# Four graph layers on one core: a group's softmax sums one unit later with longer rings, layer 3's biases added by VectorE and its norm scales made by GpSimd, layer 2's two norms sharing their small steps

## The reference

```python
x = norm(x + L0(x))   # q, k, v of the edges; score = exp(clip(k[src].q[dst] / sqrt(32), -5, 5)); sum(v*score) / sum(score)
x = norm(x + L1(x))   # z = (1+eps)*x + sum(x[src]); relu(z@W1+b1)@W2+b2; r = z+x; relu(norm(r)*gamma+beta)
x = norm(x + L2(x))   # h = x@W; e = leaky(a_src[src]+a_dst[dst]), self loops too; softmax over dst; + bias; norm*ln_w+ln_b
x = norm(x + L3(x))   # q,k,v with biases; k,v of an edge + edge_attr@We; softmax over dst; sum(v*alpha) + x@Ws + bs
```

## Time and profile before

| | |
|---|---|
| median of 3 runs | 5001.02 us (4994.6 to 5005.99) |
| the profiled execution | 4998.33 us, span 4996.6 us |
| TensorE busy | 4563.9 us, 91% of the span |
| TensorE's weight loads | 3506.0 us, 70% |
| VectorE busy | 3986.5 us, 80% |
| ScalarE busy | 2805.1 us, 56% |
| GpSimd busy | 2476.3 us, 50% |

### The profile page before, as it was taken

One profiled execution on the slowest core, in us unless ns is written; L12 is line 12 of the kernel. 1 busy time (PEld: TensorE's weight loads), 2 busy tenths in 40 slices (PEclk: granted clock), 3 DMA queues, 4 the chain that ended last, 5 costly groups with the idle time before them and its releaser, 6 DMA issues. The chain is left out here.

```text
span 4996.6 us, 90737 instructions
## 1 busy us (share of the span) xinstructions
PE 4563.9 (91%) x21673; PEld 3506.0 (70%) x21722; DVE 3986.5 (80%) x13147; ACT 2805.1 (56%) x6326; POOL 2476.3 (50%) x2462
## 2 busy tenths in 40 slices
PE   4999998779999999999888888888799999699998
PEld 3666664448888888888767777777566666577777
DVE  4777778979999999999859999999855555567666
ACT  1787886545555555555547777777611111366565
POOL 3555551237777777777466666666365554000000
PEclk8999996569999999999979999999899999899999
DMA  6777778954444444444468888787555554677775
GB/s 138 210 225 222 223 223 257 298 187 135 150 152 153 149 148 152 153 153 148 143 184 252 244 244 244 243 243 243 183 172 163 163 164 146 193 228 228 223 228 160
DMA packets 911233, 970.10 MB, mean 194 GB/s; under 512 B 104899, under 2 KB 867258, under 8 KB 910892
## 3 DMA queue, kind: packets, MB, share of 16 engines
q1 hardware_dynamic: 500692, 471.58, 32.9%
q10 hardware_dynamic: 327416, 315.35, 18.6%
q0 software_dynamic: 82784, 179.41, 12.3%
HBM read 654.56 MB, written 363.57 MB: 204 GB/s over the span
## 5 line engine op out<-in xcount | busy, mean ns | idle before, releaser
L1186 POOL DMA_INDIRECT nodes_near_rows<-hh_d,source_row x392 | 394.9, 1007 | 401.3 <-DVE nodes_weighted L1403 292.6
L586 POOL DMA_INDIRECT layer_xg<-in_x,edge_rows x392 | 386.7, 987 | 358.5 <-PE layer_t_ps L627 241.5
L884 POOL DMA_INDIRECT nodes_near_rows<-x_d,nodes_cur x392 | 419.0, 1069 | 238.2 <-POOL nodes_cur L879 170.8
L1542 POOL DMA_INDIRECT edges_xg<-x_d,edge_rows x392 | 372.9, 951 | 264.3 <-PE edges_x_ps L1568 172.6
L485 ACT ACTIVATE nodes_x<-nodes_outer_rows,nodes_outer_shift,nodes_outer_rstd 128x256 f32<-128x256 f32 x784 | 428.0, 597 | 61.1 <-issue 51.4
L1597 ACT ACTIVATE edges_xT<-edges_x_ps 128x512 f32<-128x512 f32 x196 | 117.1, 597 | 524.7 <-PE edges_x_ps L1568 524.7
L1806 PE MATMUL nodes_agg<-w_s,nodes_xT 128*128 128x256 f32 x1568 | 405.5, 381 | 0.0
L1004 PE MATMUL nodes_h_ps<-w_h,nodes_x2T 128*128 128x272 f32 x1568 | 392.2, 393 | 8.1 <-ACT nodes_x2T L1081 8.1
L660 PE MATMUL layer_agg<-layer_msg,layer_hot 128*128 128x264 f32 x784 | 314.2, 540 | 73.5 <-issue 65.7
L642 PE MATMUL layer_kv_ps<-w_kv,layer_xT 128*128 128x512 f32 x784 | 372.3, 597 | 1.0 <-DVE layer_made L751 1.0
L994 PE MATMUL nodes_out_ps<-w_b,nodes_hid 128*128 128x256 f32 x1568 | 371.2, 380 | 1.4 <-DVE nodes_inner_rows L925 0.8
(11 more groups left out here) (223 smaller groups left out, 12341.3 us busy)
## 6 DMA issues: line engine op xcount, KB each, us to landing
nodes_xin<-x_d SPq DMA_DIRECT2D x588, 256.0 KB, 3.8
layer_msg<-msg_d SPq DMA_DIRECT2D x392, 132.0 KB
hh_d<-nodes_hh ACTq DMA_DIRECT2D x196, 264.0 KB, 4.1
nodes_msg<-msg_d SPq DMA_DIRECT2D x392, 132.0 KB, 3.1
x_d<-layer_y ACTq DMA_DIRECT2D x196, 256.0 KB, 3.8
x_d<-nodes_x2b ACTq DMA_DIRECT2D x196, 256.0 KB, 3.5
nodes_hin<-hh_d SPq DMA_DIRECT2D x196, 256.0 KB, 3.9
x_d<-nodes_x ACTq DMA_DIRECT2D x196, 256.0 KB
```

The costliest lines, as they stand in the source:

```text
L586: gp.indirect_dma_start(out=xg[:, c % 8, k, :], out_offset=None, in_=x, in_offset=bass.IndirectOffsetOnAxis(ap=edge_rows[:, c, k:k + 1], a ...
L884: gp.indirect_dma_start(out=near_rows[:, r, h, :], out_offset=None, in_=x1_d, in_offset=bass.IndirectOffsetOnAxis(ap=cur[:, r, h:h + 1], a ...
L1186: gp.indirect_dma_start(out=near_rows[:, u % NR, h, :], out_offset=None, in_=hh_d, in_offset=bass.IndirectOffsetOnAxis(ap=source_row[:, 2 ...
L1542: gp.indirect_dma_start(out=xg[:, c % 8, k, :], out_offset=None, in_=x3_d, in_offset=bass.IndirectOffsetOnAxis(ap=edge_rows[:, c, k:k + 1] ...
```

## The change

- prepare: the attention columns, `gin`, the identity into `w3_s` and the split of biases leave this stage, as do the seven loads for them and for layer 3's biases. Only layer 2's bias is still split. VectorE converts the targets first and the sources behind the first mask.
- layer0: that work is done in twelve pieces, `weights(piece)`, one per VectorE step from step 61 on; its inputs are three loads at the head of ScalarE's queue. The DMAs into `pairs` go from the head of SP's queue to units 8 to 15, and their users from step 11 to step 29. `w0_kv` and `w0_q` are freed after the stage.
- nodes2: from the group's sum on, every lag grows by one. `NR` goes from 16 to 20, `HOT` from 18 to 20, `XR` from 9 to 8. The inner norm of one unit and the outer norm of the unit three behind it share one square root, one reciprocal and one shift; the root stands behind `e_row` in ScalarE's queue, the reciprocal behind `own` in VectorE's, the shift behind the inner statistics. The copy of `near_score` is two where a group wraps around the ring.
- edges3: layer 3's biases are loaded as rows at the head of SP's queue, the bias matmul is gone, and VectorE adds `kv_bias` in PSUM ahead of the join.
- nodes3: the bias matmul is gone and VectorE adds `root_bias` to `agg` in place, ahead of the statistics. GpSimd makes the one-hots and, in four small operations with a power of −0.5, the norm's scale and shift; ScalarE's root is gone. The group's sum and shares come a step later, and the transpose of the shares goes from the head of TensorE's step at lag 15 to the end of the step at lag 16.

The diff, cut:

```diff
-                for k in (1, 0):
-                    ve.wait_ge(edges_in[k], 48)
-                    nc.vector.tensor_copy(ends_f[:, k, :, :], ends_c[:, k, :, :]).then_inc(cast, 1)
-                for k in (1, 0):
-                    last = nc.vector.tensor_copy(pairs[:, :, :, k], ends_c[:, k, :, :])
-                last.then_inc(paired, 1)
+                ve.wait_ge(edges_in[1], 48)
+                nc.vector.tensor_copy(ends_f[:, 1, :, :], ends_c[:, 1, :, :]).then_inc(cast, 1)
+                nc.vector.tensor_copy(pairs[:, :, :, 1], ends_c[:, 1, :, :])
...
+                    if mask is below_lo:
+                        ve.wait_ge(edges_in[0], 48)
+                        nc.vector.tensor_copy(ends_f[:, 0, :, :], ends_c[:, 0, :, :]).then_inc(cast, 1)
+                        nc.vector.tensor_copy(pairs[:, :, :, 0], ends_c[:, 0, :, :]).then_inc(paired, 1)
...
-                link(nc.vector.tensor_tensor(b3[:, 0:D], b3[:, 0:D], rows["L2_gnn_ln_b"][0:3, :], ALU.subtract))
...
-        MASKS = U0 + 6
+        MASKS, WEIGHTS = U0 + 24, U0 + 56
...
-                sp.wait_ge(lists_out, 16)
-                for h in range(H):
-                    sp.dma_start(pairs[h * 2 * GU:(h + 1) * 2 * GU, 0:WHOLE, :],
-                                 windows[0:WHOLE * 2 * GU, :].rearrange("(g w) x -> w g x", w=2 * GU)).then_inc(pairs_in, 16)
-                    sp.dma_start(pairs[h * REST:(h + 1) * REST, WHOLE, :], windows[WHOLE * 2 * GU:TILES, :]).then_inc(pairs_in, 16)
                 for u in range(UNITS):
+                    if 8 <= u < 8 + H:
+                        h = u - 8
+                        sp.wait_ge(lists_out, 16)
+                        sp.dma_start(pairs[h * 2 * GU:(h + 1) * 2 * GU, 0:WHOLE, :],
+                                     windows[0:WHOLE * 2 * GU, :].rearrange("(g w) x -> w g x", w=2 * GU)).then_inc(pairs_in, 16)
+                        sp.dma_start(pairs[h * REST:(h + 1) * REST, WHOLE, :], windows[WHOLE * 2 * GU:TILES, :]).then_inc(pairs_in, 16)
...
+                for k, name in enumerate(("L2_gnn_att_src", "L2_gnn_att_dst")):
+                    act.dma_start(att[:, k, :], row(a[name], D)).then_inc(more_in, 16)
+                for k, name in enumerate(split_biases):
+                    act.dma_start(b3[:, k * D:(k + 1) * D], row(a[name], D, 3)).then_inc(more_in, 16)
...
+                def weights(piece):
+
+                    if piece == 0:
+                        ve.wait_ge(more_in, (2 + BV) * 16)
+                        link(nc.vector.tensor_tensor(b3[:, 0:D], b3[:, 0:D], rows["L2_gnn_ln_b"][0:3, :], ALU.subtract))
+                        nc.vector.tensor_scalar(gin[:, :], gin[:, :], 1.0, None, ALU.add)
+                    elif piece <= 2 * KC:
+                        k, j = (piece - 1) // 2, (piece - 1) % 2
+                        link(nc.vector.tensor_tensor(wprod[:, :], w2_h[:, k, 0:D], att[:, j, :], ALU.mult))
+                        link(nc.vector.tensor_reduce(watt[:, k, j * H:(j + 1) * H],
+                                                     wprod[:, :].rearrange("p (h c) -> p h c", h=H), axis=AX.X, op=ALU.add))
...
+                    if WEIGHTS <= s < WEIGHTS + 12:
+                        weights(s - WEIGHTS)
...
-        NR, HR, XR, WR, HOT, LATER = 16, 5, 9, 4, 18, 12
+        NR, HR, XR, WR, HOT, LATER = 20, 5, 8, 4, 20, 12
...
-                    g = at(14)
+                    g = at(15)
...
-                    tops, shares = (g // GU if g is not None and g % GU == 0 else None for g in (at(12), at(13)))
-                    u = at(19)
-                    if u is not None:
-                        norm_invert(ve, inner, (None, 8, u))
-                    u = at(22)
-                    if u is not None:
-                        norm_invert(ve, outer, (None, 8, u))
-                    u = at(19)
-                    if u is not None:
-                        norm_shift(ve, inner, (None, 8, u))
-                    u = at(22)
-                    if u is not None:
-                        norm_shift(ve, outer, (None, 8, u))
+                    tops, shares = (g // GU if g is not None and g % GU == 0 else None for g in (at(12), at(14)))
...
+                    if at(20) is not None or at(23) is not None:
+                        b, of = two_norms(s - 1, at(20), at(23))
+                        ve.wait_ge(rooted, s - 19)
+                        nc.vector.reciprocal(rstd[:, b, of, :], dev[:, b, of, :]).then_inc(inverted, 1)
...
+                    if at(20) is not None or at(23) is not None:
+                        b, of = two_norms(s - 1, at(20), at(23))
+                        ve.wait_ge(inverted, s - 19)
+                        nc.vector.scalar_tensor_tensor(shift[:, b, of, :], moments[:, b, of, :, 0], -1.0, rstd[:, b, of, :], ALU.mult, ALU.mult)\
+                            .then_inc(shifted, 1)
...
-                        norm_root(act, inner, (None, 8, u))
...
-                        norm_root(act, outer, (None, 8, u))
+                    if at(19) is not None or at(22) is not None:
+                        b, of = two_norms(s, at(19), at(22))
+                        if at(19) is not None:
+                            act.wait_ge(inner_merged, at(19) + 1)
+                        if at(22) is not None:
+                            act.wait_ge(outer_merged, at(22) + 1)
+                        nc.scalar.activation(dev[:, b, of, :], moments[:, b, of, :, 1], ACT.Sqrt, bias=eps_ln[:, :]).then_inc(rooted, 1)
...
+                for k, name in enumerate(("L3_gnn_bk", "L3_gnn_bv")):
+                    sp.dma_start(kv_bias[:, k * D:(k + 1) * D], row(a[name], D)).then_inc(bias_in, 16)
+                sp.dma_start(q_bias[:, :], row(a["L3_gnn_bq"], D)).then_inc(bias_in, 16)
...
-                        nc.tensor.matmul(kv_ps[r][:, :], ones3[:, :], bias3[:, 2 * D:4 * D], start=True, stop=False)
...
+                    c = at(2)
+                    if c:
+                        of_chunk = kv_ps[ring(c, 4)]
+                        ve.wait_ge(kv_done, num(c) + 1)
+                        nc.vector.tensor_tensor(of_chunk[:, :], of_chunk[:, :], kv_bias[:, :], ALU.add).then_inc(kv_biased, 1)
...
+            @blk.gpsimd
+            def _(gp):
+                link = chained(gp, small)
+                link(gp.memset(minus_half[:, :], -0.5))
+
+                def body(s, at):
+                    u = at(16)
+                    if u is not None:
+                        if u >= 4:
+                            gp.wait_ge(summed, u - 3)
+                        for h in range(2):
+                            last = gp.tensor_scalar(hot[:, u % 4, h, :], iota[:, :], target_rel[:, 2 * u + h:2 * u + h + 1], None, ALU.is_equal)
+                        last.then_inc(hot_ready, 1)
+                    u = at(20)
+                    if u is not None:
+                        b = u % 4
+                        gp.wait_ge(ln["merged"], u + 1)
+                        if u >= 4:
+                            gp.wait_ge(ln["normed"], u - 3)
+                        link(gp.tensor_scalar(ln["spread"][:, b, :], ln["moments"][:, b, :, 1], LN_EPS, None, ALU.add))
+                        link(gp.tensor_tensor(ln["rstd"][:, b, :], ln["spread"][:, b, :], minus_half[:, :], ALU.pow))
+                        link(gp.tensor_tensor(ln["back"][:, b, :], ln["moments"][:, b, :, 0], ln["rstd"][:, b, :], ALU.mult))
+                        gp.tensor_scalar(ln["shift"][:, b, :], ln["back"][:, b, :], -1.0, None, ALU.mult).then_inc(ln["shifted"], 1)
+                run_units(UNITS, 20, body)
...
-                        norm_invert(ve, ln, (None, 8, u))
-                    u = at(15)
-                    if u is not None:
-                        if u >= 4:
-                            ve.wait_ge(summed, u - 3)
-                        one_hot_halves(ve, (None, 8, u), 4, hot, hot_ready)
-                    u = at(20)
-                    if u is not None:
-                        norm_shift(ve, ln, (None, 8, u))
-                    u = at(16)
+                        if u == 0:
+                            ve.wait_ge(bias_in, 16)
+                        ve.wait_ge(summed, u + 1)
+                        nc.vector.tensor_tensor(in_halves(agg[u % 4]), in_halves(agg[u % 4]), both(root_bias), ALU.add).then_inc(based, 1)
...
-                    g = group(15)
-                    if g is not None:
-                        n = of_group(g) * H
-                        pe.wait_ge(share_ready, g + 1)
-                        if g:
-                            pe.wait_ge(weighed, GU * g)
-                        nc.tensor.transpose(share_ps[:, 0:n], share[0:n, :], ident[0:n, 0:n]).then_inc(share_turned, 1)
...
-                            nc.tensor.matmul(to, ones3[:, :], bias3[:, D:2 * D], start=False, stop=False)
...
+                    g = group(16)
+                    if g is not None:
+                        n = of_group(g) * H
```

(5 more changed lines are left out.)

260 lines of the change are left out of this document (144 added, 116 removed).

## The result

The changed kernel takes 4829.9 us (median of 4 runs, 4822.56 to 4838.49), the kernel before 4999.9 us beside it (4 runs): a ratio of 0.966, 95% interval 0.9641 to 0.968. The forecast was 4811 us. The profiled execution took 4828.96 us, span 4827.2.

The account below looks back on a forecast made before the run. TensorE was taken to bound layer0's first part, edges3 and most of nodes3, VectorE layer0's second part and, as busiest, nodes2. 4998.3 − 16 − 13 − 42 − 89 − 30 = 4808, plus 2.7 to the median: 4811 us, range 4745 to 4875.

Parts of the forecast that it names:

- Both terms: prepare: VectorE's tail moves to layer0 (−12 us), and its idle wait for the source list goes (−4 us).
- The mechanism and the size: layer0: pairs copies leaving SP's queue head end TensorE's stops of 4.1 and 7.9 us; −13 us with clock recovery.
- The matmul's price: edges3: dropping the 512-column bias matmul saves 0.216 us in each of 196 chunks, 42.4 us.
- Part (c): nodes3: VectorE stays about level, ScalarE loses the square root, and the replacement on GpSimd is hidden below 3.03 us.
- part (b): nodes3: share transpose at the end of a 3 us step ends TensorE's 1.9 us stop per group, 46 us.
- TensorE's own 24.5 us a group: nodes3: TensorE's issue time per group, two share transposes included, against 28.4 us before; 95 us over 24.5 groups.
- GpSimd's 2.4 us per unit: nodes3: estimated time of the compares and small norm operations queued on GpSimd, bounds 1.0 to 4.2 us.
- The rival that decides from 3.03: nodes3: GpSimd's chain becomes the bound from 3.03 us per unit; at 4.5 us the kernel takes 5099 us; chance 0.06.
- Two remain, taken at 0.2: nodes2: of VectorE's four small norm operations (0.37 us) two remain at 0.2, its normal step going from 4.35 to 4.18.
- The normal step: nodes2: TensorE's own 4.38 us step, through ScalarE's copies of the one work bank, stays, so normal steps gain nothing.
- clock holds: nodes2 rival: TensorE's clock no longer falls, 74 us gained, 44 more than forecast; kernel 4767 us; chance 0.2.
- nodes2 gives nothing: Part of a rival: nodes2's heavy steps stay as long and layer0's traffic only moves; about 4851 us; chance 0.17.

Follow-up runs that it names:

- the last pair of runs: Fastest nodes2 order (own, reciprocal late, merges early) on the changed kernel, without and with layer0's pairs copies back at SP's queue head: 4753.8 and 4764.6 us.
- add waits: Changed kernel, but GpSimd's nodes2 add waits for VectorE's shift and both statistics merges stand right behind the scaling by ln_w: 4791.5 us, ratio 0.9579.
- own late: Changed kernel, but in nodes2 VectorE issues inner statistics, reciprocal, outer statistics, shift, then own, with both merges behind the ln_w scaling: 4820.9 us, ratio 0.9581.
- merges early: Changed kernel's nodes2 with both statistics merges right behind the ln_w scaling, run only with other edits; with GpSimd's add waiting for the shift 4791.5 us.
- the waiting add alone: Changed kernel with one wait more: GpSimd's nodes2 add begins only after VectorE's shift of the same step; 4833.4 us, ratio 0.9611.

## Why the prediction was right, and where it was not

**prepare** (−16, measured −18.1). Both terms held. VectorE begins on the tiles of the targets at 9.74 instead of 16.36, and its last conversion, of the first edges, starts at 33.01 instead of 39.82: 6.8 us, where I counted 4 and bounded by 7.2. The loads and the barrier behind it take 4.2 us, where I took 3.

**layer0** (−13, measured −11.8). The mechanism and the size held: 10.9 us go with the copies into pairs, by the last pair of runs. What the work moved from prepare costs there was not measured by itself.

**edges3** (−42, measured −38.0). The matmul's price held: zeros put back cost 42.0 (196 x 0.216 is 42.3, not 42.4). What was missing is at the head. TensorE begins 8.3 us after the barrier instead of 6.8, and its first k, v matmuls take 3.27 us instead of 1.88: in the stage's first 16 us the granted clock is 0.50, and it was 0.66 before. The three bias loads start beside the gathers there; that they are what holds the first gathers back was not tested.

```profile
3573.20 0.42 SPq L1594 DMA_DIRECT2D edges_q_bias<-in_L_gnn_bq  x1
...
3580.27 1.09 PE L1616 MATMUL edges_x_ps<-ident,edges_xg 128*128 128x128 f32 x4 [24.14 <-DMA edges_xg<-x_d,edge_rows]
...
3585.06 3.27 PE L1631 MATMUL edges_kv_ps<-w_kv,edges_xT 128*128 128x512 f32 x4
```

**nodes3** (−89, measured −91.6). The sum is right, two of its steps are not. The bias matmuls (43) are confirmed at 42.5 us, and taking the share transpose back to its old place (46) costs 40 to 41. Part (c) I had costed at nothing, hidden work in exchange for hidden work. Taken back alone it costs 43 us: VectorE's step again begins with a wait for the root, its weighted product comes late, and TensorE stops for it ahead of the share transpose, at the new place too (19.0 us in 540), and for the copy of x behind the root (7.5). So part (b)'s "the stop goes", because a step is longer than 1.9 us, was not true of the place alone; it needed (c). The three prices add up to some 126 us and the stage gained 92, because each is what one edit is worth when the other two are there, and (b) and (c) end the same stop. The sum came out by some luck, because I had bounded it by TensorE's own 24.5 us a group, and 24.45 is where it went. GpSimd's 2.4 us per unit became 2.55 (500.1 / 196), and with what lies between its operations 2.86: in 540 us it waited only 34.6 for a merge, (540 − 34.6) / 177. The power alone takes 0.72 of it. The rival that decides from 3.03 was nearer than the 0.06 said.

**nodes2** (−30, measured −10.9). Here the failed step is one that I had in hand. I had cited the Trainium skill ("SBUF — State Buffer", section "Who interferes with whom") against part (c), found the two-input operations of nodes3 harmless, and did not ask the same of nodes2, where GpSimd's add of x reads SBUF for 1.26 us in every step and the edit moved VectorE's shift, both of whose inputs are in SBUF, from ahead of `own` to behind it, that is from before GpSimd's add to inside it. The trace and the runs agree with that rule: 0.715 us against 0.144, 85 us of VectorE's time, and nodes2 shorter by 43 us (add waits) and 50 us (own late), merges early in both, when the overlap is taken away. Of these the waiting add alone gives 1.1 us a group (42.3 to 41.2), some 27 us; the rest comes with the other edits of those kernels and at the stage's ends. The trace of the kernel before had the sign too, in the 16 long shifts above. "Two remain, taken at 0.2" is the term that was mis-sized: they take 0.16 and 0.62 us (103.3 / 168).

The rest of the working in nodes2 stands worse than its total. The forecast had a group shorter by 1.4 us and its light steps as long as before. By the table above the three lightest steps got 0.9 us longer together, and the other five 1.9 us shorter. The normal step was not held at 4.38 us by TensorE: it went up to 4.68 with the stretched shift, and some went down to 4.12 where the add waits. The lag and the rings alone were worth some 24 us. The clock was wrong as well: it was to fall once a group as before, and it fell 10 times in 21 groups. That is half of what the rival "clock holds" asked for, and the stage was not shorter for it than forecast. The range held the time because its upper side had room for "nodes2 gives nothing", and the forecast is near because prepare, edges3 and nodes3, 147 of its 190 us, came out at 148 together.

What remains open: why `own` behind the statistics and the reciprocal with it shortens the other five steps by 2 us a group was not taken apart, nor which of lag and rings gives the first 24 us.

## What to carry to other kernels

When an edit moves a small VectorE operation, write down what GpSimd does at its new place. In this kernel an operation of four elements with both inputs in SBUF ended with GpSimd's add, 0.57 us late as a rule in the changed kernel (0.715 against 0.144) and up to 1.5 us late in the kernel before (1.70 against 0.16); away from that add it took 0.14 to 0.16. Beside the issue of a gather on GpSimd it was mostly short (312 of 323 shifts in nodes2 of the kernel before; the other 11 ended with the add that followed). And an operation that looks hidden by its engine's busy share may be holding what waits for it, on another engine or behind it in the same queue: price it by taking it back alone, and don't add up prices of edits that lift the same bound.

## What the runs showed of the hardware that was not expected

- GpSimd's elementwise power of two elements per partition takes 0.72 us, a compare of 128 columns 0.61, each other small operation 0.20 to 0.24; between two dependent ones 0.07 to 0.09 us pass.
- The kernel before took 28 to 33 us longer on two of the chips than on the others. In the changed kernel's stages: layer0 1022 to 1028 us against 1009 to 1011, edges3 622 against 610, nodes2 1120 against 1109 to 1116, while nodes1 (1413 to 1416) and nodes3 (645 to 647) did not differ. In nodes2 the extra time lies at the stage's start: from the first gather to the first `own` it is 60 to 63 us on those chips and 48 to 49 on the others, and the groups behind it are as long. In layer0's head it is in idle stretches of 8 to 10 us that nothing in the profile ends. Their cause was not sought.
